# Attention and expert layer on one core: extra products ahead of the attention loop, and the value products in two halves

## The chip, the core and the metric

One Trainium2 chip, one core. The metric is the device time of one execution of the program in microseconds (us), the median of several runs.

## The reference

An adaptive layer-norm block over x of shape (2, 1024, 128), in float32:

```
mod = silu(c) @ wmod           # six vectors a batch: sa, ca, ga, sb, cb, gb; |ga|, |gb| at least 0.25
h = layernorm(x) * (1 + ca) + sa
x = x + ga * attention(h)      # 16 heads of 8, keys and values from a 64 wide latent, rotary tables
h = layernorm(x) * (1 + cb) + sb
x = x + gb * experts(h)        # 4 rounds; 4 experts 128 -> 512 -> 128, the top 2 weighted by softmax
```

A query sees the keys of its own page of 32 tokens and of those before it. The softmax runs over the scores divided by the root of 8.

## The kernel before, in words

The program has three blocks, each with an engine barrier at its end: `prep`, `attention`, `ffn`. Their engines' streams are written out by hand and meet through semaphores.

**prep** goes through four chunks of 512 tokens. For a chunk TensorE (loop at L440) makes the latent (L444), q and rotated q (L449, L450), k and rotated k (L452, L453), and the values (L459). VectorE's `rotate(c)` multiplies with the rotary tables and adds (L365 to L372); TensorE's next q products wait for its reads of the k products (`rot_read`). ScalarE and GpSimd split q and k into a leading and a trailing piece (L298, L329), and SyncE stores them to DRAM (`store_rows`) and, once batch 0 is stored, issues the loads of the first two head groups (`load_group`, L206). On VectorE `bounded` (L375 to L380) for the gate ga stands between `rotate(1)` and `rotate(2)`, and `bounded` for gb with the two products L414 and L415 between `rotate(2)` and `rotate(3)`. wog = wo * ga is needed by the output projection of the attention, gb_diag in ffn.

**attention** works on 8 groups of 4 heads (a batch has 4). Each group has 10 units (`UNITS`): pieces of at most 512 query columns against 128 keys. A head's largest scores, two rows of them, must be known before its scores are made: TensorE fills a bin (`fill_bin`, L776) for two heads, VectorE takes its maxima (L665), 20 bins a group; `turn_maxima` (L831) transposes them, VectorE copies them to mrow (L675), and SyncE writes them into the queries' extra rows. The **lead** is the stretch ahead of the loop: 28 bins, ten units of group 0 and four (`LEAD`) of group 1, and one turn. Then come 80 **steps**. Step k has two quad halves: `quad(k, 0)` and `quad(k, 1)`. A half makes the scores of two heads (L757, into a ring of 3 PSUM banks) and fills one bin of the group that is `NU + LEAD` steps ahead (ring of 2); the second half is preceded by `keep_busy`, two products of 128x512 into the bin's bank whose result is overwritten (L790; called fillers). ScalarE takes the exponential of each head's scores (L633), four a step, in order. `score_room` lets a pair of scores start when the exponential three places before the pair's second is done, so the second half waits for the first exponential of its own step, and the first half for the third of the step before. Behind both halves stands `weigh(k - 1)`: the value products of the step before, four heads side by side in 32 columns each (L821), which wait for all four of that step's exponentials. At the end of a unit list (`LAST_UNIT`: units 2 and 9, the short ones with 256 columns) ScalarE copies the sums out (L640).

The last 14 steps have no bins and no fillers. From step 68 on (`FIRST_TILE`) `project` stands between the halves: transposes to tokens (L844), VectorE's divide (L707, L709), transpose back (L852), output product with wog (L859). PE's stream of a step before:

```
quad(k, 0)
project(k - FIRST_TILE)
quad(k, 1)
if k >= 1:
    weigh(k - 1)
if turn_due(k + NU + LEAD) is not None:
    turn_maxima(turn_due(k + NU + LEAD))
```

**ffn** is untouched.

Of the kernel before, what the change touches and what calls it, by code (L numbers as in the profile page):

```python
# [13 lines left out]
P = 128  # L14
# [70 lines left out]
PAIR_HEADS = [2, 0]  # L85
BUSY_FIRST, BUSY_LATER, BUSY_LAST = 2, 2, 3

# [35 lines left out]
def adaln_block(nc, w, out):  # L123

    with ExitStack() as stack:
# [27 lines left out]
        with ExitStack() as upto_attention:  # L153
# [5 lines left out]
            m.pieces = [ma.sb(f"pieces_{s}", [P, NCH, 2, CH], F32R) for s in "qk"]  # L159
            m.pieces_out = ma.sem("pieces_out")  # L160
            with ExitStack() as part:
                prep(nc, m, Mem(nc, part))
# [56 lines left out]
def prep(nc, m, l):  # L219
# [7 lines left out]
    wv = l.sb("wv", [LAT, E])  # L227
    wo = l.sb("wo", [E, E])
    cos, sin = l.sb("cos", [P, T]), l.sb("sin", [P, T])
    xn = l.sb("xn", [P, NT, E])  # L230
    lat = l.sb("lat", [LAT, 2, CH])
    ga = l.sb("ga", [P, B, E])
    gt, gs = l.sb("gt", [P, B, E]), l.sb("gs", [P, B, E])
    bt, bs = l.sb("bt", [P, B]), l.sb("bs", [P, B])
    rc = [l.sb(f"rc{s}", [P, CH]) for s in "qk"]
# [8 lines left out]

    in_c, in_mod, in_w, in_wo, in_tab, in_rows = (
        l.sem(n) for n in ("in_c", "in_mod", "in_w", "in_wo", "in_tab", "in_rows"))
    in_x = [l.sem(f"in_x{c}") for c in range(NCH)]
# [8 lines left out]
    with nc.Block() as block:  # L256

        @block.sync
        def _(sp):
            x_dram = w["x"].rearrange("b (t p) e -> p (b t) e", p=P)  # L260
            for c in range(NCH):
                sp.dma_start(m.x[:, TPC * c:TPC * (c + 1), :], x_dram[:, TPC * c:TPC * (c + 1), :]).then_inc(in_x[c], 16)
                if c == 0:
                    for dst, name in ((wq, "wq"), (wd, "w_down"), (wk, "wk_up"), (wv, "wv_up")):
                        sp.dma_start(dst[:, :], w[name]).then_inc(in_w, 16)
            sp.dma_start(wo[:, :], w["wo"]).then_inc(in_wo, 16)
            for rows, dst in ((w["k_rows"], m.kp), (w["q_rows"], m.qp)):
                sp.dma_start(dst.rearrange("g h r t -> (g h) r t")[:, ROW_MAX:HROWS, :],
                             rows.rearrange("(a r) t -> a r t", a=1).broadcast_to([GROUPS * HG, HROWS - ROW_MAX, T]))\
                    .then_inc(in_rows, 16)  # L270
            for c in range(TPB):
                sp.wait_ge(piece0, 2 * (c + 1))
                sp.wait_ge(piece1, 2 * (c + 1))
                store_rows(sp, m, c)
            sp.wait_ge(in_rows, 32)
            sp.wait_ge(pieces_out, 16 * 2 * TPB * TERMS)
            load_group(sp, m, 0, 0)
            load_group(sp, m, 1, 1)
# [54 lines left out]
        def _(v):  # L333
# [39 lines left out]

            def bounded(g, t, s):
                link(nc.vector.tensor_scalar(t, g, -1.0, None, ALU.mult))  # L375
                link(nc.vector.tensor_tensor(t, t, g, ALU.max))
                link(nc.vector.tensor_scalar(t, t, 0.25, None, ALU.max))
                link(nc.vector.tensor_scalar(s, g, 0.0, 2.0, ALU.is_ge, ALU.mult))
                link(nc.vector.tensor_scalar(s, s, -1.0, None, ALU.add))
                link(nc.vector.tensor_tensor(t, t, s, ALU.mult))  # L380

            v.wait_ge(exp_c, 1)
# [11 lines left out]
            for dst, src in ((wqs, wq), (wks, wk)):  # L394
# [3 lines left out]
            s.then_inc(swap_ok, 1)  # L398
            nc.vector.tensor_copy(ga[:, :, :], pmod[:, E:E + B * E].rearrange("p (b e) -> p b e", b=B))\
                .then_inc(mod_read, 1)  # L400
# [6 lines left out]
            rotate(1)  # L407
            v.wait_ge(mod_read, 2)
            bounded(ga[:, :, :], gt[:, :, :], gs[:, :, :])
            rotate(2)  # L410
            bounded(m.modc[:, 5, :], bt[:, :], bs[:, :])
            v.wait_ge(in_wo, 16)
            for b in range(B):
                nc.vector.tensor_tensor(m.wog[:, b, :], wo[:, :], gt[:, b, :], ALU.mult)  # L414
                nc.vector.tensor_scalar(m.gbd[:, b, :], m.ident[:, :], bt[:, b:b + 1], None, ALU.mult)  # L415
            rotate(3)

        @block.tensor
        def _(pe):
# [20 lines left out]
            for c in range(NCH):  # L440
# [21 lines left out]
                if c == 0:  # L462
                    turn(1)


def attention(nc, m, l):
# [11 lines left out]
    w2_raw = l.sb("w2_raw", [P, NE * FF // P, E])  # L478
    w1_raw, rec, att, att_t, xn = m.w1_raw, m.rec, m.att, m.att_t, m.xn
    st = l.ps("st", [P, ST_RING, CH])  # L480
    ov = l.ps("ov", [P, CH])
# [10 lines left out]
    dve, stat_ok, var_ok, refined, xn_ok, ht_ok, h_ok, hi_ok, cur_ok = (  # L492
        l.sem(n) for n in ("dve_proj", "stat_ok", "var2_ok", "refined", "xn2_ok", "ht_ok", "h2_ok", "hi0_ok", "cur0_ok"))

    CHAIN = 3
# [28 lines left out]
    with nc.Block() as block:  # L524
# [132 lines left out]
        def _(v):  # L657
# [38 lines left out]
            def link(ins):  # L696
# [3 lines left out]
                v.wait_ge(dve, links[0])  # L700

            def divide(t):
                v.wait_ge(heads_ok, t + 1)
# [20 lines left out]
            def moments(t):  # L724
                v.wait_ge(stat_ok, t + 1)
                link(nc.vector.bn_aggr(m.mv[:, t, :], m.stats[:, t, :]))

            for step in range(TILES + 3):
# [12 lines left out]
        def _(pe):  # L741
# [44 lines left out]
            def keep_busy(k, slot):  # L786

                keys = m.ks[k // NU % SLOTS]
                for i in range(BUSY_FIRST if k < NU else BUSY_LATER):
                    nc.tensor.matmul(mx[:, slot, i, :], keys[:, 0:P], keys[:, 0:CH], start=True, stop=True)  # L790
# [16 lines left out]

            def weigh(k):

# [3 lines left out]
                c, blocks = UNITS[u]  # L813
                pe.wait_ge(exp_done, HG * (k + 1))
                if u == 0:
                    pe.wait_ge(vs_ok, g + 1)
                if u in FIRST_UNIT and 2 * g + c > 0:
                    pe.wait_ge(ov_read, 2 * g + c)
                for j, off, q0, nq in blocks:
                    for h in range(HG):  # L820
                        mm = nc.tensor.matmul(ov[32 * h:32 * h + 32, q0:q0 + nq],  # L821
                                              vs[s][:, j, h, :], probs[k % PROBS][:, h, off:off + nq],
                                              start=u in FIRST_UNIT, stop=u in LAST_UNIT,
                                              skip_group_check=True)
                mm.then_inc(pv_done, 1)

# [27 lines left out]

            def wo(t):
                pe.wait_ge(att_sb, t + 1)
                if t >= 1:
# [10 lines left out]
            def project(step):  # L868
# [6 lines left out]
                if 2 <= step <= TILES + 1:  # L875
                    wo(step - 2)

            for unit in range(NU + LEAD):
                for pair in range(PAIRS):
                    fill_bin(unit // NU, PAIRS * (unit % NU) + pair)  # L880
                if turn_due(unit) is not None:
                    turn_maxima(turn_due(unit))
            for k in range(STEPS):
                quad(k, 0)
                project(k - FIRST_TILE)
                quad(k, 1)
                if k >= 1:
                    weigh(k - 1)
                if turn_due(k + NU + LEAD) is not None:
                    turn_maxima(turn_due(k + NU + LEAD))  # L890
            for step in range(STEPS - FIRST_TILE, TILES + 2):
                project(step)
            weigh(STEPS - 1)
            for _ in range(BUSY_LAST):
# [533 lines left out]
```

## Time and profile before

| | us |
|---|---|
| median of 3 runs | 717.0 (711.28 to 720.33) |
| the profiled execution | 711.26 |
| its span in the profile | 709.5 |
| TensorE busy in the span | 660.5 (93%) |
| VectorE busy | 572.2 (81%) |
| ScalarE busy | 506.4 (71%) |
| GpSimd busy | 193.7 (27%) |

The profile is one execution. Busy time says how long an engine had work in it, not that it set the pace; PEclk is the granted clock of TensorE as a share of full speed. PE is TensorE's products, DVE VectorE, ACT ScalarE, POOL GpSimd, SPq the queue of SyncE. In a timeline row stand start, duration of the merged instructions, engine, line, operation, output<-inputs, shapes, count, and in brackets the idle time before it and what ended it. Products overlap, so two rows' durations may run into each other; starts give the pace. Products in f32 show as two instructions each.

### The profile page before, as it was taken

What the parts mean: (1) busy time and instruction counts of PE and PEld (TensorE: products, weight loads), DVE (VectorE), ACT (ScalarE), POOL (GpSimd) and SP (SyncE); (2) the same over time, 40 slices, a digit from 0 to 9 for tenths busy, and PEclk for the clock granted to TensorE, in tenths of its full rate; (3) what the DMA queues carried; (4) which work ended last, traced back from release to release, by engine and by line L of the source; (5) the groups of instructions that cost most, each with busy time, mean ns of one, the idle gap of its engine ahead of it and who ended that gap; (6) DMA issues with size and microseconds to landing.
All of it is one profiled execution on the core that took longest, in us unless ns stands there. A gap on an engine that the chain in (4) does not pass through costs nothing.

```text
span 709.5 us, 11157 instructions
## 1 busy us (share of the span) xinstructions
PE 660.5 (93%) x4007; PEld 440.2 (62%) x4007; DVE 572.2 (81%) x973; ACT 506.4 (71%) x907; POOL 193.7 (27%) x208
## 2 busy tenths in 40 slices
PE   6957799999999989989988999999999999999996
PEld 3424434434444435567766777877787778778884
DVE  7869888887888863578988898889888988888775
ACT  1410277787787787777777788888888888888883
POOL 0240800000000000434272442444244424422222
PEclk9955599999999999999999999999999999999998
DMA  7279001101101000011011110111011101110101
GB/s 276 92 242 319 4 2 62 58 6 64 59 5 63 4 1 4 1 61 60 1 61 60 61 60 15 48 60 61 5 56 61 60 2 59 61 61 2 74 16 30
DMA packets 16902, 40.64 MB, mean 57 GB/s; under 512 B 2832, under 2 KB 8208, under 8 KB 14736
## 3 DMA queue, kind: packets, MB, share of 16 engines
q1 hardware_dynamic: 16128, 38.42, 15.7%
q10 hardware_dynamic: 720, 1.51, 0.6%
q8 instruction: 32, 0.52, 0.3%
q14 instruction: 22, 0.18, 0.1%
HBM read 32.19 MB, written 9.57 MB: 59 GB/s over the span
## 4 chain that ended last, share of the span: by engine, by line
PE 34%; DVE 13%; issue 5%; ACT 3%; POOL 1%; POOLq 0%; DVEq 0%; ACTq 0%
DVE gel_lo L1160 7%; PE y L1003 6%; PE y L1005 5%; PE y L1004 5%; PE hid L992 5%; PE hid L993 5%; PE hid L994 5%; DVE part L1216 2%; ACT gel_hi L1119 2%; PE plog L1018 2%; ACT gel L1118 1%; PE pcw L1029 1%; DVE at_least L1186 1%; DVE cw L1205 0%; DVE at_least L1188 0%
## 5 line engine op out<-in xcount | busy, mean ns | idle before, releaser
L1160 DVE TENSOR_TENSOR gel_lo<-gel,gel_hi 128x512 fp32r<-128x512 f32 x256 | 241.6, 978 | 9.1 <-ACT gel_hi L1119 7.8
L633 ACT ACTIVATE probs<-st 128x512 f32<-128x512 f32 (+1 forms) x320 | 160.4, 555 | 86.1 <-PE st L757 82.3
L665 DVE TENSOR_REDUCE mcol<-mx 128x2 f32<-128x1024 f32 (+2 forms) x160 | 176.7, 1118 | 36.2 <-PE mx L776 33.9
L1118 ACT ACTIVATE gel<-hid,b_sb 128x512 f32<-128x512 f32 x256 | 176.0, 687 | 38.3 <-PE hid L994 18.8
L1119 ACT ACTIVATE gel_hi<-hid,b_sb 128x512 fp32r<-128x512 f32 x256 | 174.7, 682 | 0.0
L1336 POOL TENSOR_TENSOR cur<-cur,part 128x512 f32<-128x512 f32 x64 | 106.1, 1658 | 239.4 <-DVE part L1216 239.3
L1003 PE MATMUL y<-gel_hi,w_hi 128*128 128x512 f32 x256 | 105.6, 413 | 3.3 <-DVE gel_lo L1160 3.3
L776 PE MATMUL mx<-ks,qs 30*128 30x128 f32 (+4 forms) x576 | 90.4, 392 | 13.3 <-DVE mcol L665 8.9
L992 PE MATMUL hid<-pieces_q,w_hi 128*128 128x512 f32 x256 | 101.7, 397 | 0.5 <-PEq L524 0.5
L994 PE MATMUL hid<-pieces_q,w_lo 128*128 128x512 f32 x256 | 101.6, 397 | 0.0
L993 PE MATMUL hid<-pieces_q,w_hi 128*128 128x512 f32 x256 | 101.5, 397 | 0.0
L1004 PE MATMUL y<-gel_hi,w_lo 128*128 128x512 f32 x256 | 101.3, 396 | 0.0
L1005 PE MATMUL y<-gel_lo,w_hi 128*128 128x512 f32 x256 | 101.1, 395 | 0.0
L757 PEld LDWEIGHTS st<-qs,ks 26*128 26x128 f32 (+1 forms) x576 | 45.5, 187 | 83.2 <-ACT probs L633 36.7
L757 PE MATMUL st<-qs,ks 30*128 30x128 f32 (+4 forms) x576 | 82.8, 356 | 7.3 <-ACT probs L633 4.7
L1216 DVE SCALAR_TENSOR_TENSOR part<-y,b_sb,pieces_k 128x512 f32<-128x512 f32 x64 | 47.9, 748 | 47.5 <-PE y L1005 47.4
L821 PE MATMUL ov<-probs,vs 128*32 128x512 f32 (+3 forms) x768 | 79.2, 500 | 0.0
L776 PEld LDWEIGHTS mx<-ks,qs 24*128 24x128 f32 (+1 forms) x576 | 48.6, 207 | 22.3 <-DVE mcol L665 17.1
L1003 PEld LDWEIGHTS y<-gel_hi,w_hi 128*128 128x128 f32 x256 | 48.3, 188 | 17.5 <-DVE gel_lo L1160 5.5
L992 PEld LDWEIGHTS hid<-pieces_q,w_hi 128*128 128x128 f32 x256 | 48.0, 187 | 12.7 <-issue 0.9
L994 PEld LDWEIGHTS hid<-pieces_q,w_lo 128*128 128x128 f32 x256 | 48.1, 188 | 12.2
L993 PEld LDWEIGHTS hid<-pieces_q,w_hi 128*128 128x128 f32 x256 | 48.1, 188 | 11.4
(160 smaller groups left out, 588.7 us busy)
## 6 DMA issues: line engine op xcount, KB each, us to landing
pieces_k<-gate_rows SPq DMA_DIRECT2D x16, 1024.0 KB, 4.6
ks<-k_rows SPq DMA_DIRECT2D x8, 512.0 KB, 3.8
qs<-q_rows SPq DMA_DIRECT2D x8, 512.0 KB, 4.7
q_rows<-pieces_q SPq DMA_DIRECT2D x12, 256.0 KB, 3.0
k_rows<-pieces_k SPq DMA_DIRECT2D x12, 256.0 KB, 4.0
x_sb<-in_x SPq DMA_DIRECT2D x4, 256.0 KB, 6.9
k_rows<-in_k_rows SPq DMA_DIRECT2D x1, 1024.0 KB, 8.7
q_rows<-in_q_rows SPq DMA_DIRECT2D x1, 1024.0 KB, 9.9
```

The source lines that it names most:

```text
L633: nc.scalar.activation(probs[k % PROBS][:, h, 0:n], st[:, (HG * k + h) % ST_RING, 0:n], ACT.Exp, scale=SCALE).then_inc(exp_done, 1)
L665: nc.vector.tensor_reduce(mcol[g % 2][:, PAIR_HEADS[pair]:PAIR_HEADS[pair] + 2, slot:slot + step * (len(blocks) - 1) + 1:step], mx[:, at % ...
L776: mm = nc.tensor.matmul(mx[:, at % MX_RING, i, off:off + w], m.qs[s][r0:r0 + rows, t * P:(t + 1) * P], m.ks[s][r0:r0 + rows, k0:k0 + w], s ...
L992: nc.tensor.matmul(h, m.w1_hi[:, e, f], cur_hi[:, c, :], start=True, stop=False)
L993: nc.tensor.matmul(h, m.w1_hi[:, e, f], cur_lo[:, c, :], start=False, stop=False)
L994: nc.tensor.matmul(h, m.w1_lo[:, e, f], cur_hi[:, c, :], start=False, stop=True).then_inc(hid_ok, 1)
L1003: nc.tensor.matmul(o, m.w2_hi[:, x, :], gel_hi[n % RING][:, :], start=first, stop=False)
L1004: nc.tensor.matmul(o, m.w2_lo[:, x, :], gel_hi[n % RING][:, :], start=False, stop=False)
L1005: nc.tensor.matmul(o, m.w2_hi[:, x, :], gel_lo[n % RING][:, :], start=False, stop=last).then_inc(y_ok, 1)
L1118: nc.scalar.activation(gel[n % RING][:, :], hid[n % RING][:, :], ACT.Gelu_apprx_tanh, bias=bias)
L1119: nc.scalar.activation(gel_hi[n % RING][:, :], hid[n % RING][:, :], ACT.Gelu_apprx_tanh, bias=bias).then_inc(gel_ok, 1)
L1160: nc.vector.tensor_tensor(gel_lo[n % RING][:, :], gel[n % RING][:, :], gel_hi[n % RING][:, :], ALU.subtract).then_inc(lo_ok, 1)
```

## The change

Four parts. (1) VectorE's `bounded` operations, wog and gb_diag leave prep and stand in attention, behind the last group's maxima and ahead of the first divide; ga and wo live on into attention, the temporaries lie in w2_raw, and the first output product waits for wog. (2) At the end of prep's TensorE stream stand five 128x512 f32 products, and one at the start of attention's. (3) In the lead every bin is followed by one 256 column f32 product, and the turn by one of 512; they write ov, which nothing has used yet. (4) In the loop `weigh` is cut in two: one half of its columns (or of its two blocks) between the quad halves, ahead of `project`, with the wait for the exponentials; the other behind the second half, and it signals pv_done. `keep_busy` issues one product in full units from step 10 on, two in the first ten steps and in units 2 and 9.

```diff
@@ constants
-BUSY_FIRST, BUSY_LATER, BUSY_LAST = 2, 2, 3
+BUSY, BUSY_LAST = 256, 3
+BUSY_PREP, BUSY_START, BUSY_TURN = 5, 1, 1
+BUSY_SHORT, BUSY_FULL = 2, 1
+
+def halves(blocks):
+    if len(blocks) == 2:
+        return [blocks[:1], blocks[1:]]
+    (j, off, q0, nq), = blocks
+    return [[(j, off, q0, nq // 2)], [(j, off + nq // 2, q0 + nq // 2, nq // 2)]]
@@ prep: DVE
             rotate(1)
-            v.wait_ge(mod_read, 2)
-            bounded(ga[:, :, :], gt[:, :, :], gs[:, :, :])
             rotate(2)
-            bounded(m.modc[:, 5, :], bt[:, :], bs[:, :])
-            v.wait_ge(in_wo, 16)
-            for b in range(B):
-                nc.vector.tensor_tensor(m.wog[:, b, :], wo[:, :], gt[:, b, :], ALU.mult)
-                nc.vector.tensor_scalar(m.gbd[:, b, :], m.ident[:, :], bt[:, b:b + 1], None, ALU.mult)
             rotate(3)
@@ prep: PE, behind the loop over chunks
+            for _ in range(BUSY_PREP):
+                nc.tensor.matmul(turned[0][:, :], m.ident[:, :], m.cur[:, 0, :], start=True, stop=True)
@@ attention: DVE, behind keep_rows(GROUPS - 1), ahead of the divides
+            v.wait_ge(w_lo, NE)
+            bounded(m.ga[:, :, :], gt, gs)
+            bounded(m.modc[:, 5, :], bt[:, :], bs[:, :])
+            v.wait_ge(m.in_wo, 16)
+            for b in range(B):
+                nc.vector.tensor_tensor(m.wog[:, b, :], m.wo[:, :], gt[:, b, :], ALU.mult).then_inc(wog_ok, 1)
+                nc.vector.tensor_scalar(m.gbd[:, b, :], m.ident[:, :], bt[:, b:b + 1], None, ALU.mult)
@@ attention: PE
             def keep_busy(k, slot):
                 keys = m.ks[k // NU % SLOTS]
-                for i in range(BUSY_FIRST if k < NU else BUSY_LATER):
+                for i in range(BUSY_SHORT if k < NU or k % NU in LAST_UNIT else BUSY_FULL):
                     nc.tensor.matmul(mx[:, slot, i, :], keys[:, 0:P], keys[:, 0:CH], start=True, stop=True)
-            def weigh(k):
+            def weigh(k, part):
...
-                pe.wait_ge(exp_done, HG * (k + 1))
-                if u == 0:
-                    pe.wait_ge(vs_ok, g + 1)
-                if u in FIRST_UNIT and 2 * g + c > 0:
-                    pe.wait_ge(ov_read, 2 * g + c)
-                for j, off, q0, nq in blocks:
+                if part == 0:
+                    pe.wait_ge(exp_done, HG * (k + 1))
+                    if u == 0:
+                        pe.wait_ge(vs_ok, g + 1)
+                    if u in FIRST_UNIT and 2 * g + c > 0:
+                        pe.wait_ge(ov_read, 2 * g + c)
+                parts = halves(blocks)
+                for j, off, q0, nq in parts[part]:
                     for h in range(HG):
...
-                                              start=u in FIRST_UNIT, stop=u in LAST_UNIT,
+                                              start=u in FIRST_UNIT and part == 0, stop=u in LAST_UNIT,
                                               skip_group_check=True)
-                mm.then_inc(pv_done, 1)
+                if part == 1:
+                    mm.then_inc(pv_done, 1)
             def wo(t):
+                if t == 0:
+                    pe.wait_ge(wog_ok, B)
...
+            for _ in range(BUSY_START):
+                nc.tensor.matmul(ov[:, :], m.ident[:, :], m.cur[:, 0, :], start=True, stop=True)
             for unit in range(NU + LEAD):
                 for pair in range(PAIRS):
                     fill_bin(unit // NU, PAIRS * (unit % NU) + pair)
+                    nc.tensor.matmul(ov[:, 0:BUSY], m.ident[:, :], m.cur[:, 0, 0:BUSY], start=True, stop=True)
                 if turn_due(unit) is not None:
                     turn_maxima(turn_due(unit))
+                    for _ in range(BUSY_TURN):
+                        nc.tensor.matmul(ov[:, :], m.ident[:, :], m.cur[:, 0, :], start=True, stop=True)
             for k in range(STEPS):
                 quad(k, 0)
+                if k >= 1:
+                    weigh(k - 1, 0)
                 project(k - FIRST_TILE)
                 quad(k, 1)
                 if k >= 1:
-                    weigh(k - 1)
+                    weigh(k - 1, 1)
...
-            weigh(STEPS - 1)
+            for part in range(2):
+                weigh(STEPS - 1, part)
```

The rest of the diff moves ga, wo and their semaphore to the outer scope, `bounded` into attention, and adds the semaphore wog_ok.

## Rows read from the trace of the kernel before

**Rows 1.** Busy time by stage; the first line names the columns.
```profile
core 0: us, PE busy (x) PEld busy (x) DVE busy (x) ACT busy (x) POOL busy (x), PEclk, DMA share, GB/s
35.00:40.00 5.00, 2.94 (x6) 0.82 (x4) 4.76 (x11) 1.98 (x4) 1.67 (x2) 0.85 0.93 293
50.00:81.60 31.60, 21.83 (x109) 12.41 (x109) 29.01 (x30) 0.00 (x0) 11.69 (x21) 0.50 0.64 202
81.60:90.00 8.40, 7.53 (x44) 3.79 (x44) 5.55 (x5) 4.34 (x8) 7.42 (x9) 0.52 0.01 2
90.00:264.00 174.00, 167.87 (x1674) 75.15 (x1674) 144.88 (x141) 134.76 (x273) 5.25 (x19) 1.00 0.10 33
```

**Rows 2.** Timeline of prep: start us, us, engine, line.
```profile
30.17 0.29 DVE L375 TENSOR_SCALAR gt<-ga 128x256 f32<-128x256 f32 x1
...
30.67 1.02 PE L450 MATMUL pq<-cur,wqs 128*128 128x512 f32 x2
...
34.29 0.69 DVE L365 TENSOR_TENSOR rcq<-pq,cos 128x512 f32<-128x512 f32 x1
...
37.55 1.18 PE L449 MATMUL pq<-cur,wq 128*128 128x512 f32 x2 [2.06 <-DVE rsk L366]
...
38.78 0.15 DVE L375 TENSOR_SCALAR bt<-modc 128x2 f32<-128x2 f32 x1
...
41.72 0.68 DVE L365 TENSOR_TENSOR rcq<-pq,cos 128x512 f32<-128x512 f32 x1
```

**Rows 3.** Start of attention: timeline, landing, first step.
```profile
41.46 0.43 SPq L206 DMA_DIRECT2D qs<-q_rows  x1
...
49.91 0.92 PE L776 MATMUL mx<-ks,qs 30*128 30x128 f32 x8 [4.06 <-PEq L256]
...
qs<-q_rows SPq DMA_DIRECT2D x1, 512.0 KB, 4.5
...
81.69 0.47 PE L757 MATMUL st<-qs,ks 30*128 30x128 f32 x2 [0.18 <-DMA qs<-mrow]
```

**Rows 4.** A full step of the loop, PE and ACT; fillers by duration.
```profile
151.32 0.50 PE L757 MATMUL st<-qs,ks 26*128 26x512 f32 x2
...
151.81 0.73 PE L790 MATMUL mx<-ks 128*128 128x512 f32 x2
152.51 0.50 PE L757 MATMUL st<-qs,ks 26*128 26x512 f32 x2
...
152.99 1.06 PE L821 MATMUL ov<-probs,vs 128*32 128x512 f32 x8
153.99 0.50 PE L757 MATMUL st<-qs,ks 26*128 26x512 f32 x2
...
142.77 1.09 ACT L633 ACTIVATE probs<-st 128x512 f32<-128x512 f32 x2 [0.16 <-PE st L757]
...
151.86 2.26 ACT L633 ACTIVATE probs<-st 128x512 f32<-128x512 f32 x4 [0.34 <-PE st L757]
...
L790 PE MATMUL mx<-ks x132: 387/496/796, 82.5 to 259.7; 128*128 128x512 f32 x132
```

**Rows 5.** PE: step 10, values of 384 + 128 and of 256 columns.
```profile
111.26 0.33 PE L757 MATMUL st<-qs,ks 30*128 30x128 f32 x2
...
145.06 1.07 PE L821 MATMUL ov<-probs,vs 128*32 128x384 f32 x16
...
301.76 0.64 PE L821 MATMUL ov<-probs,vs 128*32 128x256 f32 x8
```

**Rows 6.** Steps with the projection: PE and DVE.
```profile
267.17 0.28 DVE L675 COPY mrow<-mx 64x128 f32<-64x128 f32 x1 [5.00 <-PE mx L831]
...
270.65 0.27 PE L852 MATMUL mx<-ident,att 128*128 128x128 f32 x1
...
285.90 0.50 PE L757 MATMUL st<-qs,ks 26*128 26x512 f32 x2
...
287.25 0.50 PE L757 MATMUL st<-qs,ks 26*128 26x512 f32 x2
```

More of the change, by code:

```diff
@@ L160, in adaln_block @@
             m.pieces_out = ma.sem("pieces_out")
+            m.ga, m.wo = ma.sb("ga", [P, B, E]), ma.sb("wo", [E, E])
+            m.in_wo = ma.sem("in_wo")
             with ExitStack() as part:
@@ L227, in prep @@
     wv = l.sb("wv", [LAT, E])
-    wo = l.sb("wo", [E, E])
     cos, sin = l.sb("cos", [P, T]), l.sb("sin", [P, T])
@@ L231, in prep @@
     lat = l.sb("lat", [LAT, 2, CH])
-    ga = l.sb("ga", [P, B, E])
-    gt, gs = l.sb("gt", [P, B, E]), l.sb("gs", [P, B, E])
-    bt, bs = l.sb("bt", [P, B]), l.sb("bs", [P, B])
     rc = [l.sb(f"rc{s}", [P, CH]) for s in "qk"]
@@ L243, in prep @@
     pmod = l.ps("pmod", [P, CH])
-    in_c, in_mod, in_w, in_wo, in_tab, in_rows = (
-        l.sem(n) for n in ("in_c", "in_mod", "in_w", "in_wo", "in_tab", "in_rows"))
+    in_c, in_mod, in_w, in_tab, in_rows = (l.sem(n) for n in ("in_c", "in_mod", "in_w", "in_tab", "in_rows"))
     in_x = [l.sem(f"in_x{c}") for c in range(NCH)]
@@ L265, in _ @@
                         sp.dma_start(dst[:, :], w[name]).then_inc(in_w, 16)
-            sp.dma_start(wo[:, :], w["wo"]).then_inc(in_wo, 16)
+            sp.dma_start(m.wo[:, :], w["wo"]).then_inc(m.in_wo, 16)
             for rows, dst in ((w["k_rows"], m.kp), (w["q_rows"], m.qp)):
@@ L372, in rotate @@
                     nc.vector.tensor_tensor(ro[side][:, c % 2, :], rc[side][:, :], rs[side][:, :], ALU.add).then_inc(rot, 1)
[L374 to L380, printed above, removed]
             v.wait_ge(exp_c, 1)
@@ L398, in _ @@
             s.then_inc(swap_ok, 1)
-            nc.vector.tensor_copy(ga[:, :, :], pmod[:, E:E + B * E].rearrange("p (b e) -> p b e", b=B))\
+            nc.vector.tensor_copy(m.ga[:, :, :], pmod[:, E:E + B * E].rearrange("p (b e) -> p b e", b=B))\
                 .then_inc(mod_read, 1)
@@ L479, in attention @@
     w1_raw, rec, att, att_t, xn = m.w1_raw, m.rec, m.att, m.att_t, m.xn
+    gt, gs = w2_raw[:, 0:B, :], w2_raw[:, B:2 * B, :]
+    bt, bs = l.sb("bt", [P, B]), l.sb("bs", [P, B])
     st = l.ps("st", [P, ST_RING, CH])
@@ L493, in attention @@
         l.sem(n) for n in ("dve_proj", "stat_ok", "var2_ok", "refined", "xn2_ok", "ht_ok", "h2_ok", "hi0_ok", "cur0_ok"))
+    wog_ok = l.sem("wog_ok")
     CHAIN = 3
@@ L700, in link, with bounded @@
                 v.wait_ge(dve, links[0])
+            def bounded(g, t, s):
+                link(nc.vector.tensor_scalar(t, g, -1.0, None, ALU.mult))
+                link(nc.vector.tensor_tensor(t, t, g, ALU.max))
+                link(nc.vector.tensor_scalar(t, t, 0.25, None, ALU.max))
+                link(nc.vector.tensor_scalar(s, g, 0.0, 2.0, ALU.is_ge, ALU.mult))
+                link(nc.vector.tensor_scalar(s, s, -1.0, None, ALU.add))
+                link(nc.vector.tensor_tensor(t, t, s, ALU.mult))
             def divide(t):
```

## The prediction

> **What bounds the kernel now.** I read the busy times by stage first. Between 50.0 and 81.6 us TensorE is at half clock, yet VectorE is busy 29.01 of 31.6 us: the lead ahead of the attention loop belongs to VectorE's maxima, and TensorE's clock costs it little. Between 81.6 and 90.0 us the first loop steps run at half clock (0.52). From 90 to 264 us the clock is full and TensorE is busy 167.87 of 174.00 us [rows 1]. The clock fell around 38.5 us (0.85 over 35 to 40), when TensorE had done 2.94 us of work in 5.00 [rows 1]: it stood 2.06 us for VectorE's rotation of chunk 2 [rows 2].
>
> Next the order of work in prep. The bounded gate factors (L375 to L380) and L414 and L415 sit ahead of the rotations of chunks 2 and 3 on VectorE [rows 2]. Then the start of attention: TensorE waits 4.06 us for the block's end, although its keys and queries were issued at 41.46 us and took 4.5 us [rows 3].
>
> Last the loop at full clock, one full step from 151.32 to 153.99, 2.67 us [rows 4]. Four scores and maxima products (a quad half) take 0.49, two filler products 0.70, the second half 0.48, the value products 1.00. The first exponential starts 0.53 after its scores (151.86). The second half stands 1.19 behind the first and waits for it. So the step is the chain scores, first exponential, scores, values, and the two fillers just fit into its wait. Four exponentials from 151.86 take 2.26 with the gap in their middle, and a pair 1.09 [rows 4]: ScalarE does not bound.
>
> **The change part by part.** The sum is made against the profiled execution's 711.3 us (span 709.5); the median of the runs shown is 717.0.
>
> *Prep.* Chunk 2's rotation can start when its q products end, 30.67 + 1.02 = 31.7, instead of 34.29; TensorE's wait of 2.06 goes, and the second block on VectorE, 38.78 to 41.72, goes too [rows 2]. All of prep but the new products then ends about 6 us earlier, near 43.7. The five new products on TensorE follow the last value product (about 40 us, at full clock). One such 128x512 f32 product is the pair of instructions of L450, 1.02 with its latency, about 0.86 each when they follow one another (an estimate from it) [rows 2]: 4.3 us, to 44.3; the block's end, then BUSY_START 0.86, to 45.5. What is late next is the data: 41.46 + 4.5 = 46.0 [rows 3]. First maxima product at 46.1 instead of 49.91: **-3.8**. Ends: -2 (the data or the block's end later than counted) and -5.
>
> *Lead.* 28 fillings, each now with a 256 column f32 product. At full clock a filling takes about 0.48 (a quad half [rows 4]) and that product about 0.57 (as value products of 256 columns, below): 28 times 1.05 is 29.4 us of TensorE beside VectorE's 29.01 [rows 1], so it is nearly hidden, and what VectorE still waits (31.6 - 29.0, the start among it) shrinks a little at full clock. I take **-0.5**, ends -1.5 and +1.5. With the clock down it is another case, below.
>
> *The value products in two halves.* No row shows 256 columns of a 512 unit, but unit 9 has 256: 0.64 against 1.06 for 512 [rows 4, 5], 0.42 less, so a half costs 1.00 - 0.42, about 0.57, and two cost 1.14. Lower end: 0.50, nothing extra, since a unit of 384 + 128 columns lasts 1.07, the same as one of 512 [rows 5]. I take 0.57. The Trainium skill says the same as a rule ("TensorEngine Tiling (Array Packing)", Key Properties: changing the tiling mode drains the array). It has no price; by it the step has five changes where it had four, and it speaks for the upper end. The trace agrees as far as 0.57 is more than half of 1.00.
>
> *The wait that moves.* weigh(k-1) needs the fourth exponential of step k-1. Before, it stood behind the second quad half, where that was long done. Now its first half stands ahead of it, and all of TensorE queues behind. Count from S, the start of the third exponential. The fourth ends at S + 1.09, TensorE goes on 0.05 later: 1.14. Half the values: 1.71. One filler: the second of a pair adds 0.73 - 0.39 = 0.34 [rows 4], so one leaves 0.36: 2.07. Scores to exponential 0.53: the next S at 2.60. Against 2.67, **-0.07 a full step**. The freed filler pays for the drain and the wait, and little more. Carrying the same addition through the ten steps of a group: the five full steps together -0.5; the three whose predecessors have short exponentials or 256 column values -0.2 each; the two short ones, which keep 2 fillers (0.34 more), +0.35 each. A group goes from 26.9 to 26.4. Steps 10 to 65 are 5.6 groups: **-2.5**. Ends: -6 (halves at 0.50) and +4 (a half at 0.65).
>
> *The first ten steps.* They keep two fillers everywhere: +0.34 each in eight steps, so 26.4 + 2.7 less 1.0 for step 0, which has no values: 28.1. Before: 81.69 to 111.26, 29.6 [rows 3, 5], with three steps at half clock. **-1.5**, if the clock is full. Steps 66 and 67 have neither fillers nor maxima: **-0.7**.
>
> *Steps 68 to 79,* with the projection between the quad halves and no fillers. Before, in the step at 285.90, the second quad half stands 1.35 behind the first (0.43 scores, 0.92 projection), then 0.43 and 1.00 [rows 4, 6]: 2.78, all TensorE. Now 1.14 + 0.57 + 0.92 + 0.53 = 3.16: the projection, which used to fill the wait, stands behind the first half of the values. +0.38 in a full step, less in short ones: **+3.4**. Ends 0 and +4.5.
>
> *The gate factors on VectorE, ahead of the first divide.* 16 operations, 4.1 + 2.9 = 7.0 us in prep (30.17 to 34.29 and 38.78 to 41.72), beside a busy GpSimd; 16 times the 0.15 of the narrowest is 2.4, and the wide ones take 0.29 and more [rows 2]. GpSimd rests where they go, so I take 4.2, an estimate between the ends. They start after the copy at 267.17 + 0.28; before, the first back transpose came 3.5 us after that copy's start, at 270.65 [rows 6]; with the longer step it would come at 4.4, and divide is done at 5.2: **+0.8**. Ends 0 and +3. This work is hidden in prep by nothing and here almost wholly.
>
> Sum: -3.8 - 0.5 - 1.5 - 2.5 - 0.7 + 3.4 + 0.8 = **-4.8**, so 706.5 for an execution like the profiled one. The runs of before spread from 711.28 to 720.33; the profiled one is the lowest. Part of that spread may be the clock's rise after 81 us coming later in some, which the change would cover. I put the median at **709**.
>
> **The rivals.** *The drain is free and the exponentials set the pace.* With 0.50 for a half and 0.28 for a lone filler a full step is 2.45, -0.22 in some 46 steps is -10, the tail +2, the start -6.5: 697. For it: 384 + 128 columns cost nothing more. Against: the 256 column row. *The prep gain is taken back:* the queue of stores now meets the loads of group 0, or the tail loses its upper end: 712 to 719. *Slower: the clock falls ahead of the lead and stays down through it.* TensorE still has a gap at the block's end. At half clock the streaming doubles: a filling about 0.75 and its extra product 2 times 0.42 and 0.15, together about 1.7 where 1.05 was counted, so 28 times 0.65 is +18; with the steps at half clock as before +3: 727 for the best run, 733 for the median. It is slower by over 2% from about 25 of the 28 fillings at half clock. For it: the clock did not come back in 31 us of lead at 21.83 of 31.60 busy. Against: TensorE would then be busy without a gap, and it rose in 81.6 to 90.0 at 7.53 of 8.40 [rows 1]. *The change doesn't do what it says:* the clock falls at 38.5 all the same and is full again by the lead: between forecast and no gain.
>
> **How the numbers follow.** Forecast 0.62, first rival 0.16, gain taken back 0.14, slower 0.08. Range 698 to 722: from just above the first rival to the second's upper end plus the spread of medians; the forecast's own is 702 to 714. Two per cent of 717 is 14.3 us, about what a measurement of this kernel can tell: faster means below 702.7, slower above 731.3. Faster 0.18 (the first rival and a low edge of the forecast), slower 0.08, within 0.74.
>
> **What would show it.** Clock 1.00 from 20 us to the end; first maxima product at 46; a 256 column half at 0.57 to the next instruction; a full step of 2.60 with TensorE waiting for ScalarE ahead of the first half; steps 68 to 79 longer, 3.1 to 3.2; a short wait of TensorE for the first divide. The forecast is wrong if the full step is under 2.5 or over 2.75, or the lead runs at half clock.

## The result and the profile after

The changed kernel takes 782.5 us (median of 4 runs, 769.86 to 801.63); the kernel before took 714.75 on the same chip (4 runs, 711.28 to 720.33). The ratio is 1.0867, 95% interval 1.0781 to 1.0954: slower by 8 to 10%. The forecast was 709, within 2% of before. The profiled execution took 783.76, its span is 781.9. Of most kernels here some executions are over 1.5% slower than the fastest, and all ratios leave those out, so they are not the quotient of the medians. All four executions of the changed kernel ran long at half clock: their mean granted clock is 0.858 to 0.914, that of the profiled execution before 0.960.

The first thing to see is the profile page's line of the granted clock, 40 slices of 19.5 us (PEclk: tenths of full speed):

```profile
PEclk9999999655559855559999999999999999999999
```

Half clock (1.2 GHz of 2.4) lies in slices 7 to 11 and 13 to 17, counted from 0: in the attention loop, where [rows 1] had 1.00 throughout, and in the steps behind it. Its exact stretches are 141.5 to 192.7, 196.1 to 233.6 and 267.8 to 349.7 us. The busy times by stage (columns as in [rows 1]):

```profile
46.00:77.00 31.00, 30.80 (x163) 16.14 (x161) 28.42 (x29) 0.00 (x0) 10.23 (x19) 1.00 0.70 230
108.40:137.60 29.20, 25.80 (x321) 12.20 (x321) 22.66 (x23) 20.82 (x43) 0.86 (x3) 1.00 0.12 39
137.60:141.50 3.90, 3.07 (x45) 1.72 (x45) 3.40 (x4) 3.21 (x8) 0.40 (x1) 0.99 0.73 268
141.50:192.70 51.20, 50.57 (x376) 21.67 (x368) 25.57 (x26) 23.61 (x50) 0.86 (x3) 0.50 0.07 22
233.70:267.70 34.00, 29.52 (x372) 14.05 (x374) 26.23 (x26) 24.30 (x50) 0.86 (x3) 1.00 0.10 33
```

The lead (first line) is as forecast: full clock, TensorE busy 30.80 of 31.00. The loop is not: at full clock TensorE is busy 25.80 of 29.20 us, where [rows 1] had 167.87 of 174.00. Then the clock falls, TensorE is busy 50.57 of 51.20, and it is the bound until the clock returns.

Step lengths, worked out from the starts of each step's first scores (units 0 to 9 of a group, then the sum of the ten; the last row is put together from several groups, since no group ran at half clock throughout):

```
before, full clock          2.65 2.86 2.41 2.45 2.81 2.67 2.67 3.06 2.85 2.44   26.9
after, steps 0-9            2.65 3.05 2.84 2.73 3.48 3.00 2.99 3.55 3.16 2.84   30.3
after, full clock           2.65 3.32 2.84 2.50 3.25 2.76 2.76 3.32 2.92 2.84   29.2
after, half clock           3.82 4.56 4.46 3.61 4.45 4.42 4.42 4.76 4.85 4.46   43.8
```

The same starts give the account, profiled execution against profiled execution, up to the first instruction of ffn (303.79 before, 377.07 after):

| stretch | before | after | difference | of it at full clock |
|---|---|---|---|---|
| to the loop | 81.7 | 78.1 | -3.6 | -3.6 |
| steps 0 to 9 | 29.6 | 30.3 | +0.7 | +0.7 |
| steps 10 to 65 | 150.2 | 210.9 | +60.6 | +12.9 |
| step 66 to ffn | 42.3 | 57.8 | +15.5 | +5.1 |

(The last column: 5 groups of 29.16 and six steps that take 17.32 together, against 150.2; for the tail the same stretch of e4 below, which ran at full clock.) So 58 us of 73 are the clock; 19 are steps that are longer at full clock, by the halves and, in the tail, the gate factors; 4 come back at the start. Of the 0.7 in steps 0 to 9 one has to know that three of these steps ran at half clock before: e5 below, with the loop of before at full clock, takes 26.8 for them.

### The profile page after: what moved, and what is told of

It reads as the page before. It is cut to its first block, busy times and chain, and to the rows that moved or that the text cites. A ratio compares the mean times of both kernels' runs of the same rounds, so it can differ in the third digit from the quotient of the medians.

```text
span 781.9 us, 12231 instructions
## 1 busy us (share of the span) xinstructions
PE 738.1 (94%) x4544; PEld 473.9 (61%) x4544; DVE 569.8 (73%) x973; ACT 506.8 (65%) x907; POOL 193.6 (25%) x208
## 4 chain that ended last, share of the span: by engine, by line
PE 31%; DVE 12%; issue 5%; ACT 2%; POOL 1%; POOLq 0%; DVEq 0%; ACTq 0%
DVE gel_lo L1187 6%; PE y L1030 5%; PE y L1032 5%; PE y L1031 5%; PE hid L1019 5%; PE hid L1020 5%; PE hid L1021 5%; DVE part L1243 2%; ACT gel_hi L1146 2%; PE plog L1045 1%; ACT gel L1145 1%; PE pcw L1056 0%; DVE at_least L1213 0%; DVE cw L1232 0%; DVE at_least L1215 0%
## 5 line engine op out<-in xcount | busy, mean ns | idle before, releaser
L837 PE MATMUL ov<-probs,vs 128*32 128x256 f32 (+2 forms) x1280 | 127.3, 480 | 5.0 <-ACT ovs L638 4.7
L771 PE MATMUL st<-qs,ks 30*128 30x128 f32 (+4 forms) x576 | 104.4, 438 | 11.5 <-ACT probs L631 8.2
L771 PEld LDWEIGHTS st<-qs,ks 26*128 26x128 f32 (+1 forms) x576 | 59.5, 242 | 78.4 <-issue 55.7
L790 PE MATMUL mx<-ks,qs 30*128 30x128 f32 (+4 forms) x576 | 101.5, 428 | 0.1
L790 PEld LDWEIGHTS mx<-ks,qs 24*128 24x128 f32 (+1 forms) x576 | 55.0, 229 | 10.3 <-DVE mcol L663 6.9
```

The lines of the kernel that those rows point to most:

```text
L771: mm = nc.tensor.matmul(st[:, n % ST_RING, off:off + w], m.ks[s][r0:r0 + rows, j * P:(j + 1) * P], m.qs[s][r0:r0 + rows, c * CH + q:c * CH ...
L790: mm = nc.tensor.matmul(mx[:, at % MX_RING, i, off:off + w], m.qs[s][r0:r0 + rows, t * P:(t + 1) * P], m.ks[s][r0:r0 + rows, k0:k0 + w], s ...
```

## The experiments

There were two theories on the clock. **A:** TensorE's clock was held up by the fillers; with one fewer TensorE is idle more around the steps of units 0 and 3, which make the short value products of units 9 and 2, and the clock falls just behind them. In the trace each of the three falls stands 0.7 to 1.3 us into a step of unit 1 or 4 (steps 21, 34, 54). **B:** the halves' waits, not the filler, open the idle stretches. **C**, for the tail: the stall of the gate factors ahead of the first divide lets the clock fall there. None of e1 to e12 leaves out work of the reference: the results of fillers and extra products are overwritten. Step lengths and windows are those of one profiled execution of each kernel.

**e1, two fillers in every step.**

```diff
-BUSY_SHORT, BUSY_FULL = 2, 1
+BUSY_SHORT, BUSY_FULL = 2, 2
```

> The changed kernel with two fillers in every step. Theory A (the removed filler lets TensorE's clock fall in the loop): the clock stays 1.00 through the loop; a full step is 3.00 as in the changed kernel's first ten, so a group is some 31.3 against 26.9 before, and the time is about 738. Theory B (the halves themselves, by their gaps, let it fall): the clock falls as in the changed kernel, and the time stays at 780 or above.

**e2, the kernel before with one filler** from step 10 on: no halves, nothing else of the change.

```diff
-BUSY_FIRST, BUSY_LATER, BUSY_LAST = 2, 2, 3
+BUSY_FIRST, BUSY_LATER, BUSY_LAST = 2, 1, 3
```

> The kernel before with one filler a step, value products whole. Theory A: the clock falls in the loop too, at steps 0 or 3 of a group, whose values have 256 columns; 740 to 790. Theory B: the clock stays full after it has risen, a full step stays 2.67 since it waits for the exponential anyway, 709 to 713.

e1: 738.56 (736.32 to 767.43, 6 runs), ratio 1.035 [1.0269, 1.0431]; five of its six runs have a mean clock of 0.971 to 0.996. The profiled one is the sixth: at half clock from the loop's third microsecond to 169.1, then full to the end of the loop. e2: 778.35 (767.53 to 793.65, 4 runs), ratio 1.0814 [1.0699, 1.0929]. One filler fewer a step costs nearly as much as the whole change. Windows of e2, the last stretch at full clock and what followed:

```profile
92.70:123.40 30.70, 28.55 (x292) 12.87 (x288) 25.98 (x25) 24.08 (x49) 0.86 (x3) 1.00 0.11 37
123.40:330.00 206.60, 206.34 (x1274) 84.77 (x1274) 115.97 (x113) 107.52 (x214) 3.89 (x14) 0.50 0.07 22
```

The clock falls in step 14, a unit 4, and stays down 239 us (123.4 to 362.3), over the first 206.60 of which TensorE is busy 206.34. All four runs of e2 have a mean clock of 0.815 to 0.856. That is A, and B is not needed: e2 has no halves. And e1, with halves and with the filler, holds the clock in the loop once it is up (0.99 and more in four runs).

**e4, two fillers also in units 0 and 3,** one in the other full units.

```diff
-for i in range(BUSY_SHORT if k < NU or k % NU in LAST_UNIT else BUSY_FULL):
+for i in range(BUSY_SHORT if k < NU or k % NU in LAST_UNIT + FIRST_UNIT else BUSY_FULL):
```

> The changed kernel with two fillers also in steps 0 and 3 of a group, one in the other full steps. If the clock falls only where a 256 column step comes with one filler (all three falls in the changed kernel's trace lie there): clock 1.00 through the loop, full step 2.77, about 727. If one filler in the full steps is too little by itself: falls elsewhere, 750 or more.

728.43 (728.27 to 750.38, 4 runs), ratio 1.0229 [1.015, 1.0308]. One product more in two steps of ten takes 54 us off the median of the changed kernel. Three of the four runs have a mean clock of 0.996 or more; the fourth has 0.955, so it too lost the clock for a while, where is not known. Window of e4:

```profile
100.00:255.00 155.00, 137.44 (x1676) 64.79 (x1674) 118.01 (x116) 108.08 (x219) 4.29 (x15) 1.00 0.11 37
```

Full clock with TensorE busy 137.44 of 155.00, about the average of the changed kernel ahead of its fall (25.80 of 29.20). So the average of a stretch does not tell whether the clock holds; what e4 changes is which steps have the filler. What remains against before to ffn is -3.8 at the start, +0.7 in steps 0 to 9, +15.2 in steps 10 to 65 (165.5, a group 29.57) and +5.1 in the tail: 17.

**e8, the kernel before with two fillers in units 0, 2, 3, 9 and one elsewhere:** does the same placement hold the old order?

```diff
-for i in range(BUSY_FIRST if k < NU else BUSY_LATER):
+for i in range(2 if k < NU or k % NU in LAST_UNIT + FIRST_UNIT else 1):
```

> The kernel before with one filler in the full steps and two in steps 0, 2, 3, 9 and the first ten. The value products are whole. If the clock falls where a 256 column step has one filler, as e4_two_in_0_and_3 says: no fall in the loop, a full step 2.67 as before since it waits for the exponential: 709 to 714. If one filler is too little in full steps: 730 or more.

721.73 (711.49 to 779.16, 4 runs; before in the same session 719.87), ratio 1.0031 [0.9898, 1.0164]. In the profiled run the clock is 1.00 from 92.5 us on:

```profile
92.50:260.00 167.50, 155.58 (x1589) 69.26 (x1581) 141.19 (x137) 129.83 (x262) 4.80 (x17) 1.00 0.10 34
```

But the slowest run has a mean clock of 0.849. So one run in four fell deeply, where all four of e2 did: the placement makes the fall rarer and does not exclude it. The freed time buys nothing: a full step is 2.67 as before, since ScalarE ends the wait that the filler filled.

**e3, the start alone:** the change's prep, lead and gate factors, with the loop of before (whole `weigh`, two fillers).

```diff
-BUSY_SHORT, BUSY_FULL = 2, 1
+BUSY_SHORT, BUSY_FULL = 2, 2
@@ loop, and weigh as before
-                if k >= 1:
-                    weigh(k - 1, 0)
                 project(k - FIRST_TILE)
                 quad(k, 1)
                 if k >= 1:
-                    weigh(k - 1, 1)
+                    weigh(k - 1)
```

> The changed kernel's start (gate factors moved, extra products in prep, lead and turn) with the loop as before: value products whole, two fillers. If the start gives what the changed kernel's trace shows (loop from 78.1 instead of 81.7) and its first ten steps run at full clock (25.9 instead of 29.6), less 1 for the gate factors ahead of the first divide: about 705, clock 1.00 from 18 us to the end. If the start is what makes the clock fall later: 730 or more.

713.92 (710.85 to 720.98, 10 runs), ratio 1.0016 [0.9971, 1.0061]. The loop starts at 78.06 instead of 81.69 and steps 0 to 9 gain 1.4, and more than that is given back at the tail: step 68 to ffn takes 44.2 us, before 36.7. Two rows of its timeline, VectorE's last gate operation and TensorE's first back transpose (in brackets the idle time and what ended it):

```profile
266.37 0.28 DVE L740 TENSOR_SCALAR gb_diag<-ident,bt 128x128 f32<-128x128 f32 x1
...
267.20 0.33 PE L866 MATMUL mx<-ident,att 128*128 128x128 f32 x1 [1.42 <-DVE att L715]
```

TensorE waits 1.42 us for the divide, step 69 takes 4.07 instead of 2.44, and behind it the clock is half from 269.0 to 282.7, as C has it. So 1.6 of the 7.4 us lost there are the stall, and the rest is mostly half clock.

**e5, e3 with the gate factors on GpSimd,** which rests there, in front of its split of group 1's rows; the same factors in five operations.

```diff
+            gates()               # bounded, wog, gb_diag on gpsimd
             for g in range(1, GROUPS):
                 take_apart(g)
@@ DVE
-            v.wait_ge(w_lo, NE)
-            bounded(m.ga[:, :, :], gt, gs)
...
```

> The start of the changed kernel with the loop as before (as in e3_start_alone), and the gate factors made by GpSimd in the first steps of the loop, where it idles, in five operations instead of six. Theory C (in e3_start_alone the gate factors on VectorE stall TensorE at step 69, and that stall lets the clock fall in the projection steps): step 69 back from 4.07 to 2.43, no fall behind it, and the loop and projection steps as before: 714 less 1.6 less some 6 for the four slow steps: 705 to 707. If the fall there has another cause (where the clock's count stands): the fall stays and 711 to 713.

705.06 (704.71 to 720.5, 6 runs) against 719.87, ratio 0.9878 [0.9812, 0.9943]: the best kernel of this study, and faster than before by about 1%, with five of six runs at a mean clock of 0.993 or more. Windows of e5, lead, loop, tail:

```profile
46.00:77.80 31.80, 31.60 (x168) 16.73 (x167) 29.29 (x30) 0.00 (x0) 11.01 (x19) 1.00 0.68 224
77.80:254.00 176.20, 169.77 (x1699) 76.89 (x1702) 148.54 (x144) 136.17 (x276) 19.56 (x40) 1.00 0.09 32
254.00:297.00 43.00, 40.43 (x348) 21.70 (x348) 19.46 (x85) 30.88 (x62) 10.23 (x32) 1.00 0.01 2
```

Its gain of 6.6 us up to ffn is the loop's start (77.88, -3.8) and steps 0 to 9, now all at full clock (26.76 for 29.57, -2.8); the rest up to ffn is equal to within 0.1.

**e6, e3 without any extra product:** only the gate operations moved.

```diff
-            for _ in range(BUSY_PREP):
-                nc.tensor.matmul(turned[0][:, :], ...)
@@ and the same for BUSY_START, the product behind each bin, and BUSY_TURN
```

> As e3_start_alone, gate factors moved on VectorE, but none of the extra products in prep, lead and turn. If the earlier start comes from the gate factors alone: first maxima product at 46 and the loop at 78 here too, at half clock in the lead without loss; the first ten steps 28 to 30, depending on the clock; 711 to 716. If the extra products bring it: loop at 81 or later.

717.38 (712.11 to 721.22, 4 runs), ratio 1.0041 [0.9954, 1.0128]. Windows of e6, the lead and the tail:

```profile
46.00:77.70 31.70, 21.84 (x109) 12.44 (x110) 29.07 (x30) 0.00 (x0) 10.37 (x18) 0.50 0.66 224
...
255.00:286.00 31.00, 29.63 (x175) 15.33 (x167) 12.05 (x39) 16.42 (x33) 0.46 (x2) 0.61 0.01 2
```

At half clock the lead still ends at 77.73: the earlier start comes from moving VectorE's operations out of prep, not from the products. The tail's fall is here too, but at 261.9, in step 67 and ahead of the stall in step 69, so C names at most one of its causes.

**e10 and e11, e5 without the products of the lead and the turn, and e5 without those of prep and the start.**

```diff
@@ e10: lead
                     fill_bin(unit // NU, PAIRS * (unit % NU) + pair)
-                    nc.tensor.matmul(ov[:, 0:BUSY], ...)
@@ e11
-            for _ in range(BUSY_PREP): ...
-            for _ in range(BUSY_START): ...
```

> e5_gates_on_gpsimd without the products behind each bin and behind the turn of the lead; those at the end of prep and the start of attention stay. If the lead's products are what keeps the clock: it falls in the lead, the loop still starts near 78, its first steps run at half clock as before, 3.66 and 4.54 instead of 2.65 and 2.73, and the time is 708 to 712. If fillings alone hold it: 705.

> e5_gates_on_gpsimd without the five products at the end of prep and the one at the start of attention; those of the lead stay. The prediction's slower rival in small: the clock falls in the gap near 43 and the lead begins at half clock, a filling with its product 1.7 instead of 1.1. If it rises again once TensorE has no gap (as in 81 to 90 before): within some 5 to 8 us, loop 3 to 5 later, 708 to 710. If it stays down through the lead: loop at 95 or later, 720 or more.

e10: 715.05 (708.05 to 721.46, 10 runs), ratio 0.998 [0.9931, 1.0028]. e11: 738.09 (734.63 to 755.38, 4 runs), ratio 1.0293 [1.0221, 1.0364]. Windows of e10 (lead, then the loop's first steps) and of e11 (the gap at prep's end, then the lead):

```profile
46.00:77.70 31.70, 21.55 (x110) 12.19 (x109) 29.07 (x30) 0.00 (x0) 11.10 (x19) 0.55 0.68 224
77.70:90.00 12.30, 11.48 (x74) 5.79 (x74) 6.86 (x7) 5.66 (x12) 11.62 (x15) 0.50 0.01 1
```

```profile
40.00:46.00 6.00, 0.69 (x7) 0.50 (x5) 1.88 (x3) 1.74 (x3) 3.77 (x6) 0.67 0.71 241
46.00:101.70 55.70, 55.56 (x167) 28.24 (x167) 31.58 (x30) 0.00 (x0) 17.68 (x26) 0.50 0.40 130
```

Without the lead's products the clock is down when the loop begins, at the same 77.74, and the first three steps take 12.6 us for the 7.8 of e5. Without prep's, TensorE is idle 5.31 of 6.00 us, the clock falls, and the lead with its products is a TensorE chain at half clock: the loop starts at 101.79, 24 us later. The two sets of products only work together.

e11 also bears on C. Its gate factors are on GpSimd, so nothing stalls ahead of the first divide, and yet its clock was half from 287.75 to 298.0, in steps 68 to 70, and step 68 to ffn took 41.1 us for 36.7. With e6 that makes two falls at this place that the stall did not cause. What remains of C is that all ten runs of e3 have a mean clock under 0.99, and five of six of e5 have 0.993 or more: the stall makes the fall likelier.

**e7, e4 with both halves of units 0 and 3 behind the second quad half:** what do the long steps of units 1 and 4 cost?

```diff
-                if k >= 1:
+                behind = k >= 1 and (k - 1) % NU in FIRST_UNIT
+                if k >= 1 and not behind:
                     weigh(k - 1, 0)
                 project(k - FIRST_TILE)
                 quad(k, 1)
+                if behind:
+                    weigh(k - 1, 0)
```

> e4_two_in_0_and_3 with both halves of the value products of units 0 and 3 behind the second quad half. In e4 the steps 1 and 4 of a group take 3.31 and 3.25 against 2.76 for a full step; theory D: the first half waits there for ScalarE's copy of the sums (ov_read), which stands behind four exponentials. Expected: these steps 2.8 to 2.9, a group 28.7 instead of 29.6, 728 becomes about 721. If the wait is not the cause: 728.

729.75 (723.55 to 747.13, 4 runs), ratio 1.019 [1.0084, 1.0297]. The group falls from 29.57 to 28.66, and the steps of units 1 and 4 from 3.31 and 3.25 to 2.86 and 2.81, as before. Yet the median wins nothing: in the profiled run the clock fell in steps 31 and 61, the first behind a stretch (165.5 to 169.1) with TensorE busy 2.82 of 3.60. The run with the highest mean clock (0.991) took 723.55, 5 us less than e4's. The falls again stand in steps of unit 1, although the moved wait is gone from them, so a fall does not need that wait.

**e9, e5 with the values cut in halves but both behind the second quad half:** is it the cut or the place?

```diff
                 project(k - FIRST_TILE)
                 quad(k, 1)
                 if k >= 1:
+                    weigh(k - 1, 0)
                     weigh(k - 1, 1)
```

> e5_gates_on_gpsimd with the value products cut in halves, but both halves behind the second quad half, where the whole stood. If the cut itself costs nothing (384 + 128 columns took the same as 512) and only the change of tiling between them and the moved wait do: full step 2.67, 705. If every half costs 0.57 wherever it stands: full step 2.81, about 715.

708.68 (705.1 to 720.72, 10 runs), ratio 0.9906 [0.9857, 0.9956]; profiled 705.10 against 705.02 of e5. Timeline of e9, TensorE, a full step:

```profile
117.79 0.50 PE L779 MATMUL st<-qs,ks 26*128 26x512 f32 x2
...
119.46 1.07 PE L845 MATMUL ov<-probs,vs 128*32 128x256 f32 x16
120.46 0.50 PE L779 MATMUL st<-qs,ks 26*128 26x512 f32 x2
```

Sixteen products of 256 columns take the 1.00 us of eight of 512, and the step is 2.67. The cut is free; what costs is that the halves stand apart and wait early.

**e12, e4 with the values of steps 68 and later behind the second half.**

```diff
-                if k >= 1:
+                if 1 <= k < FIRST_TILE:
                     weigh(k - 1, 0)
                 project(k - FIRST_TILE)
                 quad(k, 1)
+                if k >= FIRST_TILE:
+                    weigh(k - 1, 0)
```

> e4_two_in_0_and_3 with the value products of steps 68 to 79 all behind the second quad half. The steps with the projection take 3.15 in e4 and 2.78 before; if the moved wait and its place ahead of the projection make that: 2.78 again, e4's 728.4 becomes about 724. The stall for the gate factors at step 69 then grows from 0.5 to about 1.6.

727.45 (724.64 to 743.43, 4 runs), ratio 1.0147 [1.0081, 1.0213]. The steps from 70 on are 2.63, 2.96, 2.65 again, as before, where e4 has 2.99, 3.80, 3.10; but step 69 takes 4.07, against 3.55 in e4. There the wait for the divide shows uncovered. (The profiled run had lost some 19 us at half clock before, from 80.2 to 134.8; from step 66 on it ran at full clock.)

## Why the prediction was wrong, step by step

**The step that failed: "From 90 to 264 us the clock is full", carried over to a loop with one filler.** I priced the fillers by time alone ("The freed filler pays for the drain and the wait") and asked whether the clock falls only ahead of the lead and in it. The fillers' other work was to hold the clock. The question could have been asked from [rows 1]: TensorE was busy 96% of the loop, part of it with fillers in a wait for ScalarE (93% in e8, which has fewer), and the clock had fallen at 38.5 us, just behind a wait of 2.06. Removing fillers from a wait gives nothing back where ScalarE ends it (e8), and opens idle time. e2 shows the fall by this alone, e4 shows what mostly cures it. The half clock costs 58 of the 73 us.

**The full step: 2.60 forecast, 2.76 measured.** TensorE's timeline of one, and its second pair of exponentials:

```profile
125.73 0.50 PE L771 MATMUL st<-qs,ks 26*128 26x512 f32 x2 [0.15 <-ACT probs L631]
126.22 0.64 PE L837 MATMUL ov<-probs,vs 128*32 128x256 f32 x8
126.79 0.50 PE L804 MATMUL mx<-ks 128*128 128x512 f32 x1
127.22 0.50 PE L771 MATMUL st<-qs,ks 26*128 26x512 f32 x2
127.70 0.64 PE L837 MATMUL ov<-probs,vs 128*32 128x256 f32 x8
128.49 0.32 PE L771 MATMUL st<-qs,ks 30*128 30x128 f32 x2
```

```profile
124.99 1.08 ACT L631 ACTIVATE probs<-st 128x512 f32<-128x512 f32 x2 [0.43 <-PE st L771]
```

The half is 126.79 - 126.22 = 0.57, as taken, and it stands in two places. By the Trainium skill ("TensorEngine Tiling (Array Packing)", Key Properties) a change of the tiling mode drains the array; the trace agrees: two halves apart 1.14, side by side in e9 1.00. That it is the drain which takes the 0.14, no run separates. Two terms of the chain were too small. The forecast let the values start 1.14 after the third exponential's start; in the trace they start 126.22 - 124.99 = 1.23 after it. The first scores start at 125.73, 0.15 behind the end of the exponential that they wait for, where 0.05 had been taken, and the half stands behind the whole quad half, 0.49 later. (The fourth exponential ends at 124.99 + 1.08 = 126.07, also 0.15 ahead of the values; the rows do not tell which of the two held them.) And one filler takes 127.22 - 126.79 = 0.43, where 0.36 had been taken. So the chain is 1.23 + 0.57 + 0.43, and 0.52 from scores to exponential: 2.75, and 0.16 above the forecast.

**The wait that moved: a second one was overlooked.** With the first half went the wait for ScalarE's copy of the sums (`ov_read`, at units 0 and 3). Step 11 of the changed kernel, TensorE and ScalarE:

```profile
111.06 0.33 PE L771 MATMUL st<-qs,ks 30*128 30x128 f32 x2 [0.42 <-ACT probs L631]
111.29 0.60 ACT L638 ACTIVATE ovs<-ov 128x512 f32<-128x512 f32 x1
112.03 0.64 PE L837 MATMUL ov<-probs,vs 128*32 128x256 f32 x8 [0.42 <-ACT ovs L638]
114.38 0.33 PE L771 MATMUL st<-qs,ks 30*128 30x128 f32 x2 [0.22 <-ACT probs L631]
```

The copy ends at 111.89, all of TensorE waits 0.42 for it, and step 11 is 3.32 for 2.86. I had named the queue behind the wait for the exponentials, and not gone through the other waits in the moved block. e7 gives it alone: 0.9 a group. It stands in the steps where the clock fell, but e7 fell there without it. So a group came to 29.2 where 26.4 was forecast, and steps 10 to 65 to +12.9 at full clock against -2.5; steps 0 to 9 to 30.3 against 28.1. This wait and five full steps at 0.16 make 1.7 of the 2.8 a group; the rest lies in the other steps and was not taken apart. The forecast's own sum had a slip as well: its three terms for a group, -0.5, three times -0.2 and twice +0.35, make -0.4 and not -0.5, and five times -0.07 is -0.35.

**Steps with the projection: right.** Forecast 3.16 for a full one; TensorE's timeline of one:

```profile
357.46 0.50 PE L771 MATMUL st<-qs,ks 26*128 26x512 f32 x2
357.94 0.64 PE L837 MATMUL ov<-probs,vs 128*32 128x256 f32 x8
358.51 0.66 PE L861 MATMUL mx<-ident,ovs 128*128 128x128 f32 x4
359.43 0.50 PE L771 MATMUL st<-qs,ks 26*128 26x512 f32 x2
359.86 0.64 PE L837 MATMUL ov<-probs,vs 128*32 128x256 f32 x8
360.62 0.50 PE L771 MATMUL st<-qs,ks 26*128 26x512 f32 x2
```

360.62 - 357.46 = 3.16: 0.48 for the quad half, 0.57 for the first values, 0.92 for the projection, 0.43 for the second quad half, and 0.76 for the second values and the wait for the next scores. The whole tail at full clock is +5.1 (e4) against the forecast's +3.4 + 0.8 - 0.7 = +3.5; e12 confirms that the early half is what costs.

**Prep: right, -3.4 for -3.8.** TensorE's timeline:

```profile
35.88 1.13 PE L441 MATMUL pq<-cur,wq 128*128 128x512 f32 x2 [0.18 <-DVE rsk L373]
40.59 4.56 PE L457 MATMUL turned<-cur,ident 128*128 128x512 f32 x10
45.45 1.10 PE L898 MATMUL ov<-cur,ident 128*128 128x512 f32 x2 [0.30 <-PEq L263]
46.47 0.55 PE L790 MATMUL mx<-ks,qs 30*128 30x128 f32 x4
```

The stall of 2.06 in [rows 2] is 0.18, the five products take 4.56 (4.3 forecast), the first maxima product stands at 46.47 (46.1 forecast) instead of 49.91. The clock did not fall at 38.5. The lead takes 31.65 us for 31.78, -0.1 where -0.5 was forecast, so the loop starts 3.6 earlier and not 4.3. It goes at VectorE's pace, as e6 and e10 show.

**The gate factors on VectorE: size right, consequence half right.** VectorE's timeline, first and last gate operation and the first divide's reciprocal:

```profile
327.10 0.28 DVE L701 TENSOR_SCALAR w_raw<-ga 128x256 f32<-128x256 f32 x1
...
331.13 0.28 DVE L740 TENSOR_SCALAR gb_diag<-ident,bt 128x128 f32<-128x128 f32 x1
331.32 0.25 DVE L713 RECIPROCAL rec<-mx 128x16 f32<-128x16 f32 x1
```

331.32 - 327.10 = 4.2 us, as estimated. The +0.8 is not measured alone. At full clock, in e4, TensorE stands 0.36 us for the first divide:

```profile
283.69 0.33 PE L869 MATMUL mx<-ident,att 128*128 128x128 f32 x1 [0.36 <-DVE att L715]
```

In e3, without the halves' cover, the same operations make a stall of 1.42, a clock fall stands behind it, and the tail is +7.4. e5 takes them away, and in its profiled run the tail is that of before.

**The rivals.** "The clock falls ahead of the lead and stays down" had the right mechanism in the wrong place: it is e11 (loop 24 us late, estimated +18), not this kernel. "The drain is free" is false where the halves stand apart. "The prep gain is taken back" is what e3 does, by the tail; in the changed kernel the 3.6 us at the start stand. No rival had the loop's clock, and so the range (to 722) missed by 60.

**What stays open.** It is open why the clock comes back when it does, and why it sometimes falls at the loop's start even with two fillers (at 80.35 in e1, 80.17 in e12, 81.27 in e3) or around step 68 without a stall (e11). One run of six of e5 and two of ten of e9 have a mean clock of 0.969; where they fell is not known. Nor does a run separate the idle time from the kind of product: a filler less is both a wait left open and a full 128x512 product gone.

## What to carry to other kernels

Before removing an instruction that seems only to fill a wait, ask what the idle time it leaves does to the granted clock, in every step and above all in those that already wait longest; a profile at full clock prices it only as long as the clock stays. When a block of waits and products moves forward in an engine's queue, go through every wait in it, not only the one that the move is about. And put side work moved out of a start onto an engine that rests at its new place: here that was the difference between no change (e3, ratio 1.0016) and 1% faster (e5, 0.9878).

## What the hardware showed that I had not expected

The clock fell in a loop in which TensorE was busy 25.80 of 29.20 us with no wait longer than 0.5 us, behind a stretch of 3.07 of 3.90; in e4 it held at 137.44 of 155.00. Once down it stayed down under nearly unbroken work: 206.34 of 206.60 us in e2, 55.56 of 55.70 in e11's lead. In the kernel before it had come back with 7.53 of 8.40 [rows 1]. Being busy at half clock did not by itself bring full clock back in these runs. And cutting the value products in two is free where the halves stand side by side (1.00 us in e9) and costs 0.14 where they stand apart (1.14).
